# Adding the attention output to x and summing the second LayerNorm: from VectorE to ScalarE and GpSimd

## What is computed

```python
x = x + xattn(layernorm(x), ctx, ctx, ...)    # linear attention, 8 heads of 64
x = x + ffn(layernorm(x), ...)                # a router over 256 slots, and a gate

# inside xattn, the tokens as channels (c) and the 1024 columns as positions (n)
qh = softmax(Wq q, over the 64 of a head) * 64 ** -0.5
kh = softmax(Wk k, over the 1024 positions)
context = einsum('bhdn,bhen->bhde', kh, vh)
out = Wo einsum('bhde,bhdn->bhen', context, qh) + bo
xattn = out / max(sqrt(sum of out ** 2 over c), 1e-12) * g * sqrt(128)

# layernorm
(x - mean(x)) / sqrt(var(x) + 1e-5)
```

## Time and profile before

| | |
|---|---|
| median of 3 runs | 639.78 us (639.23 to 642.43) |
| the profiled execution: its span, first to last instruction | 638.0 us |
| PE busy | 618.3 us, 97% |
| DVE busy | 540.5 us, 85% |
| ACT busy | 416.7 us, 65% |
| POOL busy | 371.8 us, 58% |
| one batch in the steady middle | 30.74 us |

### The profile page before, as it was taken

One profiled execution on the slowest core, in us unless ns is written; L12 is line 12 of the kernel. 1 busy time (PEld: TensorE's weight loads), 2 busy tenths in 40 slices (PEclk: granted clock), 3 DMA queues, 4 the chain that ended last, 5 costly groups with the idle time before them and its releaser, 6 DMA issues.

```text
span 638.0 us, 11806 instructions
## 1 busy us (share of the span) xinstructions
PE 618.3 (97%) x3974; PEld 543.1 (85%) x3974; DVE 540.5 (85%) x757; ACT 416.7 (65%) x844; POOL 371.8 (58%) x369
## 2 busy tenths in 40 slices
PE   4999999999999999999999999999999999999896
PEld 3778888888898888888898888888888999998674
DVE  5989898998989898989898989898986844756897
ACT  5566666666676666667676766666664767674693
POOL 4954474847474747474757575665646446520394
PEclk9999999999999999999999999999999999999799
DMA  8944543444444444444445344433344100000056
GB/s 299 242 116 108 144 110 117 120 125 114 126 112 124 110 133 114 126 116 121 111 129 161 102 124 113 134 104 96 79 120 126 42 2 1 2 1 1 34 230 265
DMA packets 52010, 72.57 MB, mean 114 GB/s; under 512 B 10112, under 2 KB 42400, under 8 KB 51696
## 3 DMA queue, kind: packets, MB, share of 16 engines
q1 hardware_dynamic: 50912, 68.07, 37.1%
q0 software_dynamic: 896, 2.45, 1.2%
q10 hardware_dynamic: 144, 1.31, 0.6%
HBM read 29.85 MB, written 8.39 MB: 60 GB/s over the span
## 4 chain that ended last, share of the span: by engine, by line
PE 91%; DMA 3%; SPq 2%; DVE 1%; issue 1%; ACT 1%; POOL 0%; DVEq 0%; ACTq 0%; POOLq 0%
PE ob L505 18%; PE gm L482 17%; PE turn L466 8%; PE gm L558 4%; PE k_slot L440 4%; PE q_slot L440 4%; PE q_slot L442 4%; PE k_slot L442 4%; PE q_slot L441 4%; PE k_slot L441 4%; PE turn L558 4%; PE gm L491 2%; PE turn L513 2%; SPq L384 2%; DMA x_all<-Wvd_cols 1%; PE turn L682 1%
## 5 line engine op out<-in xcount | busy, mean ns | idle before, releaser
L969 POOL TENSOR_TENSOR qs_sb<-qs_sb,qrec 128x1024 f32<-128x1024 f32 x64 | 122.0, 1906 | 148.9 <-DVE qrec L1139 148.9
L738 ACT ACTIVATE ek<-k_slot,nkm 128x1024 f32<-128x1024 f32 x62 | 69.1, 1114 | 94.6 <-DVE nkm L1104 94.5
L505 PE MATMUL ob<-mt_sb,q_hd 128*128 128x128 f32 x1024 | 126.4, 277 | 0.6 <-ACT o_sb L760 0.5
L505 PEld LDWEIGHTS ob<-mt_sb,q_hd 128*128 128x128 f32 x1024 | 121.8, 192 | 5.2 <-issue 3.6
L482 PE MATMUL gm<-ekT,ctxT 128*128 128x256 f32 x512 | 118.2, 379 | 1.1 <-DMA ekT<-kt 1.1
L482 PEld LDWEIGHTS gm<-ekT,ctxT 128*128 128x128 f32 x512 | 97.0, 190 | 16.2 <-DMA ekT<-kt 1.5
L748 ACT ACTIVATE qs_sb<-qs_sb 128x1024 f32<-128x1024 f32 x64 | 68.6, 1071 | 31.7 <-DVE qs_sb L1128 31.7
L1104 DVE TENSOR_REDUCE nkm<-k_slot 128x1 f32<-128x1024 f32 x62 | 74.2, 1197 | 14.8 <-PE k_slot L442 14.7
L1135 DVE TENSOR_REDUCE qsum<-qs_sb 128x16 f32<-128x1024 f32 x64 | 76.9, 1202 | 4.1 <-ACT qs_sb L748 4.1
L1128 DVE TENSOR_TENSOR qs_sb<-q_slot,qm 128x1024 f32<-128x1024 f32 x64 | 78.4, 1224 | 2.2
L1111 DVE STREAM_TRANSPOSE kt<-ek 128x1024 f32<-128x1024 f32 x64 | 78.5, 1227 | 0.6 <-DMA ekT<-kt 0.6
(11 more groups left out here) (200 smaller groups left out, 1231.9 us busy)
## 6 DMA issues: line engine op xcount, KB each, us to landing
ekT<-kt SPq DMA_DIRECT2D x496, 64.0 KB, 2.0
ctx_in<-ctx_rows SPq DMA_DIRECT2D x16, 512.0 KB, 4.6
x_all<-x SPq DMA_DIRECT2D x16, 512.0 KB, 3.6
ctxT<-ctx_cols SPq DMA_DIRECT2D x16, 512.0 KB, 4.1
out<-q_hd SPq DMA_DIRECT2D x15, 512.0 KB, 2.6
Wuq_in<-Wuq_cols ACTq DMA_DIRECT2D x1, 1280.0 KB, 6.5
x_all<-values_cols POOLq DMA_DIRECT2D x1, 1024.0 KB, 8.3
ekT<-kt POOLq DMA_DIRECT2D x16, 64.0 KB, 4.3
```

The costliest lines, as they stand in the source:

```text
L505: last = nc.tensor.matmul(ob[:, (j % 4) * C:(j % 4 + 1) * C], q_hd[:, t, j * P:(j + 1) * P], mt_sb[:, b % 2, t, :], start=(t == 0), stop=( ...
L969: nc.gpsimd.tensor_tensor(e, e, qrec[:, i % 2, :].unsqueeze(2).broadcast_to([P, PAIR, DH]), ALU.mult).then_inc(q_mul, 1)
```

## The change

For the batches e below `RESIDUAL_BY_VECTOR` = 13, ACT takes the output out of turn (`o_scale`, scaled by gs, into o_sb, with the sum of each row accumulated), POOL adds it to X (`residual`, one step later, in the next period) and makes the new mean as the old mean plus that sum over 1024, and ACT makes the variance as an accumulated square of X less the mean (`square_sum`, at i = 1 of the next period). POOL's `rstd2_pow` for these batches moves from i = 0 to i = 3. The last three batches stay with DVE. q_hd, which q_copy writes, is laid out by step (its size is the same); o_square writes into a tile of its own (junk) instead of the other half of o_sb; mv1 keeps the first LayerNorm's mean of each batch. k's factor 64 ** -0.5 goes from `k_scale` into the copy that makes U at the start. SP's stream is written with the feed-forward tables as its 17th round; its transfers stand in the order they had. The reserve in SBUF for the descriptors of POOL's transfers becomes 4096 bytes.

```diff
+RESIDUAL_BY_VECTOR = B - 3
...
             def take_turn(user, b, i=0):
                 if used:
-                    before, n = used.pop()
-                    pe.wait_ge(copies[before][0], n)
-                used.append((user, copies[user][1] * b + i + 1))
+                    copied, n = used.pop()
+                    pe.wait_ge(copied, n)
+                if user is q_turn:
+                    used.append((q_copied, 4 * b + i + 1))
+                elif b < RESIDUAL_BY_VECTOR:
+                    used.append((o_back, b + 1))
+                else:
+                    used.append((x1_done, b + 1))
...
+            def o_scale(b):
+                act.wait_ge(o_T, b + 1)
+                act.wait_ge(gs_done, 1)
+                wait(act, nm2_done, b - 1)
+                nc.scalar.activation(o_sb[:, b % 2, :, :].rearrange("p j c -> p (j c)"), turn[:, :], ACT.Copy,
+                                     scale=gs[:, :], accum_out=osum[:, b % 2:b % 2 + 1]).then_inc(o_back, 1)
+
+            def square_sum(b):
+                act.wait_ge(x1_done, b + 1)
+                act.wait_ge(nm2_done, b + 1)
+                wait(act, ve2_done, b)
+                nc.scalar.activation(o_sb[:, b % 2, :, :].rearrange("p j c -> p (j c)"), X[:, b, :], ACT.Square,
+                                     bias=nm2[:, b % 2:b % 2 + 1], accum_out=ssq[:, :]).then_inc(ssq_done, 1)
...
                         k_exponential(b, i)
                     if i == 1 and 0 < b and has(b + 1):
                         ctx_high(b + 1)
+                    if i == 3 and 0 <= e < RESIDUAL_BY_VECTOR:
+                        o_scale(e)
                     qb, qi = (p, i - 2) if i >= 2 else (o, i + 2)
...
                     if i == 1 and 0 < b < B:
                         x_layernorm(b)
+                    if i == 1 and 0 <= e - 1 < RESIDUAL_BY_VECTOR:
+                        square_sum(e - 1)
...
-                        nc.scalar.copy(U[:, :, :].rearrange("p h c -> p (h c)"), turn[:, :]).then_inc(u_done, 1)
+                        nc.scalar.mul(U[:, :, :].rearrange("p h c -> p (h c)"), turn[:, :],
+                                      float(DH) ** -0.5).then_inc(u_done, 1)
...
+            def residual(b):
+                pool.wait_ge(o_back, b + 1)
+                nc.gpsimd.tensor_tensor(X[:, b, :], X[:, b, :], o_sb[:, b % 2, :, :].rearrange("p j c -> p (j c)"),
+                                        ALU.add).then_inc(x1_done, 1)
+                nc.gpsimd.tensor_scalar(mv2[:, b, 0:1], osum[:, b % 2:b % 2 + 1], 1.0 / N, mv1[:, b, 0:1], ALU.mult,
+                                        ALU.add).then_inc(mean2_done, 1)
+                pool.wait_ge(mean2_done, b + 1)
+                wait(pool, ssq_done, b - 1)
+                nc.gpsimd.tensor_scalar(nm2[:, b % 2:b % 2 + 1], mv2[:, b, 0:1], -1.0, None,
+                                        ALU.mult).then_inc(nm2_done, 1)
+
             def rstd2_pow(b):
+                if b < RESIDUAL_BY_VECTOR:
+                    pool.wait_ge(ssq_done, b + 1)
+                    nc.gpsimd.tensor_scalar(mv2[:, b, 1:2], ssq[:, :], 1.0 / N, None, ALU.mult).then_inc(mv2_done, 1)
...
                     if i == 0 and has(o):
                         mt_bias(o)
+                    if i == 0 and 0 <= e - 1 < RESIDUAL_BY_VECTOR:
+                        residual(e - 1)
...
-                    if i == 0 and has(e - 1):
+                    if i == 0 and has(e - 1) and e - 1 >= RESIDUAL_BY_VECTOR:
+                        rstd2_pow(e - 1)
+                    if i == 3 and 0 <= e - 1 < RESIDUAL_BY_VECTOR:
                         rstd2_pow(e - 1)
...
                 dve.wait_ge(k_exp, 4 * (b + 1))
+                wait(dve, mt_copied, b)
                 V.reciprocal(krec[:, :], ksum[:, b % 2, :]).then_inc(krec_done, 1)
-                dve.wait_ge(krec_done, b + 1)
-                wait(dve, mt_copied, b)
-                V.tensor_scalar_mul(kscale[:, :], krec[:, :], float(DH) ** -0.5).then_inc(kscale_done, 1)
...
-                    if i == 2 and has(e):
+                    if i == 2 and has(e) and e >= RESIDUAL_BY_VECTOR:
                         residual(e)
-                    if i == 3 and has(e):
+                    if i == 3 and has(e) and e >= RESIDUAL_BY_VECTOR:
                         statistics(e)
...
-    nc = bacc.Bacc("TRN2", target_bir_lowering=False, num_devices=1)
+    nc = bacc.Bacc("TRN2", target_bir_lowering=False, num_devices=1, dynamic_dma_scratch_size=4096)
```

More of the change, by code:

```diff
@@ L85, in attention_ffn_kernel @@
         krec = sb("krec", [P, T])
-        kscale = sb("kscale", [P, T])
         l2 = sb("l2", [P, J])
@@ L386, in move_k, with ffn_tables @@
                                         q * J * BLK:(q + 1) * J * BLK]).then_inc(k_moved[half], 16)
+            def ffn_tables():
+                for half in range(2):
+                    sp.wait_ge(k_moved[half], moved(B))
+                sp.dma_start(bu1[:, :], bu1_row.broadcast_to([P, UH])).then_inc(ffn_in, 16)
+                sp.wait_ge(q_prod, 4 * B)
+                sp.wait_ge(g_prod, 2 * B)
+                sp.wait_ge(m_prod, B)
+                for src, dst in ((Wu2_row.broadcast_to([P, UH]), Wu2[:, :]),
+                                 (bu2_row.broadcast_to([P, 1]), bu2[:, :]),
+                                 (gate_w_row.broadcast_to([P, 1]), gate_w[:, :]),
+                                 (gate_b_row.broadcast_to([P, 1]), gate_b[:, :])):
+                    sp.dma_start(dst, src).then_inc(ffn_in, 16)
+                sp.dma_start(WvuT_in[:, :], WvuT_raw).then_inc(wvu_in, 16)
             sp.dma_start(WkT_in, WkT_raw).then_inc(k_weights_in, 16)
@@ L400, in _ @@
             load_ctxT(1)
-            for b in range(B):
+            for b in range(B + 1):
                 if 2 <= b + 1 < B:
                     load_x(b + 1)
-                move_k(b, 0)
-                if b >= 2:
+                if has(b):
+                    move_k(b, 0)
+                if 2 <= b < B:
                     load_ctxT(b)
@@ L408, in _ @@
                     load_ctx(b + 2)
[L409 to L422, removed]
+                if has(b):
+                    move_k(b, 1)
+                else:
+                    ffn_tables()
             for b in range(B - BY_VECTOR):
@@ L502, in o_pair @@
                     wait(pe, o_copied, 2 * b + i // 2)
-                for j in (2 * i, 2 * i + 1):
+                by_pe = q_hd[:, i, :].rearrange("p (t n x) -> p t n x", t=T, n=2)
+                for n in range(2):
+                    j = 2 * i + n
                     for t in range(T):
-                        last = nc.tensor.matmul(ob[:, (j % 4) * C:(j % 4 + 1) * C],
-                                                q_hd[:, t, j * P:(j + 1) * P], mt_sb[:, b % 2, t, :],
+                        q = by_pe[:, t, n, :]
+                        last = nc.tensor.matmul(ob[:, (j % 4) * C:(j % 4 + 1) * C], q, mt_sb[:, b % 2, t, :],
                                                 start=(t == 0), stop=(t == T - 1))
@@ L752, in q_copy @@
                 wait(act, o_prod, 4 * (b - 1) + i + 1)
-                nc.scalar.copy(q_hd[:, :, 2 * i * P:2 * (i + 1) * P],
-                               turn[:, :].rearrange("p (t n) -> p t n", t=T)).then_inc(q_copied, 1)
+                nc.scalar.copy(q_hd[:, i, :], turn[:, :]).then_inc(q_copied, 1)
             def o_copy(b, half):
                 act.wait_ge(o_prod, 4 * b + 2 * (half + 1))
-                wait(act, o_T, b - 1)
+                wait(act, x1_done, b - 1)
+                if half == 0:
+                    wait(act, ssq_done, min(b - 1, RESIDUAL_BY_VECTOR))
                 wait(act, l2_sum, 2 * b)
@@ L766, in o_square @@
                 wait(act, rn_pow, b)
-                wait(act, o_T, b)
+                wait(act, l2_sum, 2 * b + half)
                 for j in range(4 * half, 4 * half + 4):
-                    last = nc.scalar.activation(o_sb[:, (b + 1) % 2, j, :], o_sb[:, b % 2, j, :], ACT.Square,
+                    last = nc.scalar.activation(junk[:, j % 4, :], o_sb[:, b % 2, j, :], ACT.Square,
                                                 accum_out=l2[:, j:j + 1])
                 last.then_inc(l2_sum, 1)
+            def o_scale(b):
[10 more added lines that the diff above has]
+                                     bias=nm2[:, b % 2:b % 2 + 1], accum_out=ssq[:, :]).then_inc(ssq_done, 1)
             def mt_scale(b):
                 act.wait_ge(m_prod, b + 1)
-                act.wait_ge(kscale_done, b + 1)
+                act.wait_ge(krec_done, b + 1)
                 wait(act, o_prod, 4 * (b - 1))
                 for t in range(T):
-                    last = nc.scalar.mul(mt_sb[:, b % 2, t, :], gm[:, t * C:(t + 1) * C], kscale[:, t:t + 1])
+                    last = nc.scalar.mul(mt_sb[:, b % 2, t, :], gm[:, t * C:(t + 1) * C], krec[:, t:t + 1])
                 last.then_inc(mt_copied, 1)
```

26 lines of the change are left out of this document (17 added, 9 removed).

## The result

The changed kernel takes 720.14 us (median of 4 runs, 715.51 to 722.5) beside 640.45 (639.23 to 642.43) of the kernel before on the same chip: a ratio of 1.122, 95% interval 1.116 to 1.129. The forecast was 711.5, the range 688 to 735. The profiled execution took 718.9 us, its span is 717.1.

The account below looks back on a forecast made before the run. PE was taken to bound the kernel. 50.8 (wait) + 0.9 (first matmul) + 20.8 (clock) − 1.1 (ekT) + 0.3 (b = 16) = 71.7 us on the median 639.78 gave 711.5 us, range 688 to 735.

Parts of the forecast that it names:

- what bounds the kernel: Steady batches: PE is busy for all 30.74 us, so relieving VectorE can gain only at the edges.
- the wait: PE at q's transpose, step 3, waits for ScalarE's scaling behind k's exponential: 3.91 us per batch, 50.8 us for 13.
- The 0.07: First matmul after the wait lasts 0.47 us instead of 0.40: 0.07 per batch, +0.9 us in all.
- The fourth rival: A freer VectorE makes k's maximum earlier, leaving 2 us of each wait: 666 us, chance 5%.
- the third rival: The scaling fits into ScalarE's idle time ahead of the exponential: 639 us, not slower, chance 3%.
- 13 × 1.6 = 20.8: Most of the 13 gaps bring PE's lower clock level, costing 1.6 us each, 20.8 us; bounds per gap 0 and 3.0.
- rival two: The clock stays low after each gap as long as near the end, 13 × 3.0 = 39.0: 730 us, chance 15%.
- the first rival: PE's clock holds at the upper level through the gaps, leaving the wait's price: 691 us, chance 20%.
- The later half of the second LayerNorm: On GpSimd, one instruction more and moved to step 3, it runs while GpSimd waits for mt: costs nothing.
- +0.3 for the addition at b = 16: GpSimd's added work ahead of q's scaling delays PE's transpose once, at b = 16: 0.3 us, bounds 0 and 2.9.
- −1.1 for ekT: End of the k stage: batch 12's statistics leave VectorE and PE's 1.10 us wait for ekT goes; bounds 0 and −1.1.
- ScalarE's pass: The scaling pass itself was priced at 1.11 us on ScalarE, against 1.28 for VectorE's pass.

Follow-up runs that it names:

- e4: Changed kernel with RESIDUAL_BY_VECTOR = 0, all 16 residuals and second statistics on VectorE again, the side edits kept: 639.84 us, ratio 1.0016.
- e1: Changed kernel with ScalarE's scaling out of turn placed ahead of k's exponential at step 3: 641.42 us, ratio 1.0042.
- e5: e1 with the later half of the second LayerNorm's factors put back to step 2 in the loop's last turn alone: 639.20 us, ratio 0.9986.
- e8: Changed kernel with 14 idle products ahead of q's transpose at step 3, filling PE's gap: 691.99 us, ratio 1.0791.
- e6: e1 with one added wait: PE's q transpose at step 3 also waits for VectorE's maximum of k: 659.30 us, ratio 1.0280.
- e3: Changed kernel with PE doing q's products, m and the output's products ahead of q's transpose at step 3: 656.58 us, ratio 1.0266.
- e2: Changed kernel with 28 idle products ahead of q's transpose at step 3, longer than the gap: 721.77 us, ratio 1.128.
- e7: e1 with one added wait: PE's q transpose at step 3 also waits for ScalarE's exponential of k: 685.70 us, ratio 1.0694.

## Why the prediction came out as it did

**Right: what bounds the kernel.** The medians of e4, e1 and e5 all lie within 0.5% of the kernel before, with VectorE's work of 13 batches taken off or left on. Relief of VectorE, with its work moved to the other two, is worth nothing that these runs can tell beside PE's 30.74 us a batch.

**Right: the wait, its place and its size.** A batch of 35 to 37 us and 13 waits of some 3.7 us were to show it; 35.9 to 37.4 and 3.65 came. Forecast 3.91 and 0.07 a batch, 51.7 us in all; e8 shows 3.83, 49.8 us. PE came 1.25 us after the start of the scaling, not 1.35. The 0.07 has no good source: the 0.47 us of a first product was set beside the 0.40 of a last one, and a first one takes 0.48 in the steady middle too (283.07). What follows the wait is q's transposes, which last 1.09 us in e8 in place of 1.04. The fourth rival, an earlier maximum, falls with VectorE's 3.37 us of waiting for PE. The deciding point of the third rival, the scaling ahead of the exponential or behind it, is what e1 turned round: 641.42 where that rival gave 639.

**Right in kind, too small: the clock.** "13 × 1.6 = 20.8" was taken from eight products at the kernel's start. Their pace is that of the lower level (0.44 us each; 0.43 in the changed kernel at 293, where the clock is 0.50), though the clock's column reads 1.00 from 7 to 11 us; but they don't tell how long a fall lasts. All 13 gaps lowered the clock, but they did so for two lengths of time. After seven of the waits the next batch took 37.3 us in the mean, after five 36.0 (the thirteenth has no batch like them behind it); beside e8's 34.57 that is 2.75 and 1.4 us. 12 × 2.20, with an estimate of 1.4 for the last, makes 27.8 us. The bounds named, 0 and 3.0, held; the choice within them was too near the short fall, and what happened lies between the forecast (1.6) and rival two (3.0). e8, where the clock was held up, took 692, the first rival's 691: the price of the wait alone was right.

The Trainium skill, TensorE: Matmul & The Clock Gate, section "HAM oscillation — how this bites in real kernels", describes a wait in every tile that lowers the clock in every tile. The trace agrees with 13 falls after 13 waits of 3.65 us; after 1.32 us (e6) there was none.

**Wrong: "The later half of the second LayerNorm … moved to step 3, runs while GpSimd waits for mt: nothing."** So it is in a steady period. In the loop's last turn, b = 16, it isn't: mt's bias stood behind the moved factors, and PE waited 2.07 us for it. The step that failed was to price a moved instruction in the steady state alone. e5 removes it; e1, which keeps it, has 1.0042.

**Not seen in the changed kernel: +0.3 for the addition at b = 16.** It shows where the big wait is gone: 0.95 us in e1. The −1.1 for ekT came as forecast in the changed kernel, e1, e3 and e5; e2, e6, e7 and e8 keep 0.20 to 0.88 of it.

**Weighed right: ScalarE's pass.** Forecast at 1.11 us, its 13 scalings lasted 1105 ns (1.10 in the timeline above) against VectorE's 1284. The Trainium skill, ScalarE: Activation LUTs, section "Rules for kernel authors", would have additions and multiplications on VectorE as the faster engine. For this pass, float32 from PSUM, the trace doesn't show ScalarE to be slower; but the two passes are not the same work, since VectorE's also adds X, and no run here is in bf16.

**The sum.** Forecast and measured, in us: wait 51.7 and 49.8; clock 20.8 and 27.8; ekT −1.1 and −1.1; end of the attention 0.3 and 2.1. That is 71.7 and 78.6. The median rose by 720.14 − 640.45 = 79.7; the last 1.1 lies within what runs of one kernel differ by. That it is so little is partly luck: in the single profiles only that of the kernel before has a fall of the clock near the end, and only that of the changed kernel has one near the start, behind a wait of 1.17 us for Wvd's columns (0.34 before).

## What to carry to other kernels

When an engine takes over the emptying of a buffer that another engine reuses, ask first where in its queue the new instruction stands, and what the instruction ahead of it waits for; here the same 1.1 us pass cost PE no wait ahead of k's exponential and made the kernel 12% slower behind it. A wait that recurs on TensorE can have two prices, its length and the clock after it (here 3.83 and 2.20 us a batch), and they can be told apart by filling the gap with idle products of known length. Price every moved instruction once more in the first and last turns of the loop, where the neighbours that covered it are missing.

## What was not expected of the hardware

A wait of the same length, ahead of the same work, did not always lower the clock: 2.56 us did so in six of 13 batches of e7, never twice in a row. The pause of 2.10 us near the end, which lowered it in the kernel before, left it up in the changed kernel. The pause, and the first stretches after it, there:

```profile
672.41 0.41 PE L691 MATMUL turn<-ident,w_sb 128*128 128x128 f32 x2 [2.10 <-issue]
...
672.00:673.00 1.00, 0.41 (x2) 0.20 (x2) 1.00 (x5) 0.14 (x1) 0.00 (x0) 1.00 0.03 8
673.00:675.00 2.00, 1.71 (x8) 0.97 (x8) 1.33 (x9) 1.70 (x7) 0.00 (x0) 1.00 0.00 0
```

Over the ten profiles that pause was followed within 2 us by a fall in five. Nor did the 2.07 us at o_pair lower the clock in the changed kernel, which it did in the profiles of e1, e3 and e7, three of the seven that have it. In e1 (0.78, then 0.50):

```profile
509.00:511.00 2.00, 1.73 (x12) 1.76 (x13) 1.40 (x2) 2.00 (x7) 1.36 (x2) 0.78 0.09 33
511.00:513.00 2.00, 2.00 (x11) 2.00 (x11) 0.08 (x1) 0.61 (x5) 1.84 (x1) 0.50 0.00 0
```

So one profile of a pause of about 2 to 2.6 us doesn't say whether the next execution pays for it. Why one such wait lowers the clock and the next doesn't stays open; no run here was made for it.
